# The constant products of an expert layer on Pool instead of TensorE, and a new order of DVE's steps for each expert

## What is computed

```python
xn = (x - mu) * rsqrt(var + LN_EPS) * gamma + beta
probs = softmax(xn @ Wr + br)
scores, idx = top_k(probs, 2)
full = [relu(xn @ W1_e + b1_e) @ W2_e + b2_e for each expert e]
c = einsum('ef,efh->eh', relu(b1), W2) + b2      # one row of 128 for each expert
c_total = c.sum(axis=0)
output = sum(scores * (full[idx] - c[idx] + c_total))
return residual + output
```

## Time and profile before

| | before |
|---|---|
| timed runs, median (three runs) | 3834.92 us |
| timed runs, lowest and highest | 3831.77 and 3837.63 us |
| profiled execution, its own time | 3823.62 us |
| profiled execution, span | 3821.9 us |
| mean granted clock of TensorE | 0.985 |
| PE, DVE, ACT, POOL busy | 96%, 47%, 66%, 13% |

### The profile page before, as it was taken

How to read it: one execution, slowest core, us unless ns; L and a number is a source line. 1 busy time by engine, 2 the same in 40 slices (tenths; PEclk the granted TensorE clock), 3 DMA queues, 4 the chain that set the end, 5 groups by cost and what they waited for, 6 DMA issues and landing times.

```text
span 3821.9 us, 83607 instructions
## 1 busy us (share of the span) xinstructions
PE 3665.1 (96%) x32040; PEld 1367.7 (36%) x32040; DVE 1796.6 (47%) x1809; ACT 2539.5 (66%) x2568; POOL 500.3 (13%) x1853
## 2 busy tenths in 40 slices
PE   8999999999899999999999999999999999897989
PEld 4333333334333333333333333342222223343444
DVE  3222222223377777777777777743211211443344
ACT  6999999993455555565555555479999999301321
POOL 1222222220000000000000000023322232001200
PEclk9999999999999999999999999999999999998989
DMA  6333232212111111111111110000000000000000
GB/s 194 102 83 96 79 99 81 98 72 72 58 35 38 40 38 40 38 40 38 40 38 40 39 43 1 1 23 4 4 4 4 4 30 2 17 28 0 0 13 28
DMA packets 104958, 162.88 MB, mean 43 GB/s; under 512 B 23108, under 2 KB 46048, under 8 KB 103104
## 3 DMA queue, kind: packets, MB, share of 16 engines
q1 hardware_dynamic: 104640, 158.16, 13.0%
HBM read 93.24 MB, written 64.88 MB: 41 GB/s over the span
## 4 chain that ended last, share of the span: by engine, by line
PE 76%; ACT 13%; issue 6%; DVE 4%; ACTq 1%; DMA 0%; SPq 0%; POOL 0%; DVEq 0%; POOLq 0%
PE ps L993 18%; PE ps L1018 18%; PE ps L671 10%; ACT probs L1365 7%; ACT probs L1376 5%; PE ps L603 4%; PE ps L883 3%; PE ps L493 3%; PE ps L499 3%; PE ps L1169 2%; PE ps L865 2%; PE ps L1180 2%; PE ps L1228 2%; PE ps L1242 1%; PE ps L298 1%
## 5 line engine op out<-in xcount | busy, mean ns | idle before, releaser
L1493 ACT ACTIVATE probs<-ps 128x1024 f32<-128x1024 f32 x808 | 828.3, 1025 | 586.9 <-PE ps L993 573.9
L1376 ACT ACTIVATE probs<-ps 128x1024 f32<-128x1024 f32 x1200 | 1119.4, 1032 | 50.9 <-PE ps L603 34.0
L2354 DVE TENSOR_TENSOR vbuf<-vbuf,probs 128x1024 f32<-128x1024 f32 x784 | 953.2, 1224 | 329.7 <-ACT probs L1493 329.7
L671 PE MATMUL ps<-probs,vst 128*32 128x512 f32 x6400 | 845.9, 600 | 27.1 <-ACT probs L1376 24.4
L2155 DVE COPY qs<-ps 128x512 f32<-128x512 f32 (+1 forms) x208 | 141.7, 681 | 572.4 <-PE ps L499 282.2
L1365 ACT ACTIVATE probs<-ps 128x1536 f32<-128x1536 f32 x268 | 362.0, 1624 | 9.6 <-PE ps L671 7.2
L1656 POOL CAST kst<-kb 128x128 fp32r<-128x128 f32 (+1 forms) x800 | 250.0, 313 | 746.2 <-PE ps L671 595.5
L993 PE MATMUL ps<-probs,kb 64*64 64x512 f32 x2560 | 332.2, 589 | 0.0
L1018 PE MATMUL ps<-probs,qz 64*64 64x512 f32 x2048 | 266.3, 590 | 1.8 <-DVE kb L2379 1.8
L1018 PE MATMUL ps<-probs,kb 64*64 64x512 f32 x2048 | 265.7, 589 | 0.0
L1668 POOL COPY vst<-vbuf 128x36 f32<-128x36 f32 (+1 forms) x816 | 192.4, 236 | 447.7 <-PE ps L671 441.0
(11 more groups left out here) (440 smaller groups left out, 3608.3 us busy)
## 6 DMA issues: line engine op xcount, KB each, us to landing
kv_scratch<-qs SPq DMA_DIRECT2D x192, 256.0 KB, 2.0
kb<-kv_scratch SPq DMA_DIRECT2D x72, 256.0 KB, 2.9
qz<-kv_scratch SPq DMA_DIRECT2D x56, 256.0 KB, 2.9
kb<-k_scratch SPq DMA_DIRECT2D x12, 816.0 KB, 6.9
vbuf<-in_L_ffn_W SPq DMA_DIRECT2D x32, 256.0 KB, 3.1
klo<-kv_scratch SPq DMA_DIRECT2D x32, 256.0 KB, 2.9
qs<-kv_scratch SPq DMA_DIRECT2D x32, 256.0 KB, 2.9
qz<-q_scratch SPq DMA_DIRECT2D x56, 64.0 KB, 2.1
```

Of the source, the lines that this page charges most:

```text
L671: mm = pe.matmul(ps[band, 6 + half, :], vst[:, r, band], probs[:, r, j * HT:(j + 1) * HT], start=start, stop=stop)
L1376: act.activation(probs[:, r, b * T:(b + 1) * T].rearrange("p (h n) -> p h n", h=2), ps[:, 2 * buf:2 * buf + 2, :], ACT.Exp, scale=HD8 ** - ...
L1493: act.activation(pr1[:, (u + (u == LAST1) + 2 * odd) % 4], ps[:, 2 * b:2 * b + 2, :], ACT.Exp, scale=HD64 ** -0.5)\
L2354: dve.tensor_tensor(sum1[:, odd, h], sum1[:, odd, h], e, ALU.add).then_inc(s["added"], 1)
```

## The change

Two things are changed, both in the third layer's expert part.

First, the matmuls L891 leave the experts. Pool's new function `weights8_constants` multiplies, for each expert, the second weights W2_e (128 partitions, four blocks of 128) by relu(b1_e), one value for each partition and block, and adds the product to a running sum `rbsum`; for expert 0 the product is written there directly. `rbsum` and `rbnext` lie in the free quarter of `probs`. Only then is the expert's `pick` column copied. Behind the last expert PE multiplies `rbsum` by a column of ones, four matmuls that end in column 0 of bank 7. DVE's addition of eight columns (L2547) is left out.

Second, DVE's steps are reordered. Before: weighting and sum of expert e - 1, then the four L2239 of expert e. After: weighting of e - 1, L2239 for f = 0 and 1, sum of e - 1, L2239 for f = 2 and 3. The order for m = 0 stays.

```diff
@@ PE, in expert(i, u)
-                        if h == 0 and m == 1:
-                            pe.wait_ge(s["rb_ready"], 1)
-                            for f in range(NF):
-                                pe.matmul(ps[:, 7, e:e + 1], wts[:, F + f * D:F + (f + 1) * D],
-                                          rb1[:, 0, e * NF + f:e * NF + f + 1], start=(f == 0), stop=(f == NF - 1))
@@ PE, behind the experts
             experts8(1)
+            pe.wait_ge(s["rb_ready"], 2 * E8)
+            for f in range(NF):
+                pe.matmul(ps[:, 7, 0:1], rbsum[:, f, :], ones[:, 0:1], start=(f == 0), stop=(f == NF - 1))
             pe.wait_ge(s["hid_ready"], 2 + 2 * E8 * NF)
@@ Pool, in place of weights8(1)
+            def constants8(e, u):
+
+                scales = rb1[:, 0, e * NF:(e + 1) * NF].unsqueeze(2).to_broadcast([P, NF, P])
+                kernels = vbuf[:, u * 2 * F + F:(u + 1) * 2 * F].rearrange("p (f d) -> p f d", f=NF)
+                pool.wait_ge(s[f"moe_w{u}"], e // 2 * 32 + 32 * (E8 // 2 + 1))
+                if e == 0:
+                    pool.wait_ge(s["rb_ready"], 1)
+                    pool.tensor_tensor(rbsum, kernels, scales, ALU.mult).then_inc(s["rb_ready"], 1)
+                else:
+                    pool.tensor_tensor(rbnext, kernels, scales, ALU.mult).then_inc(s["rb_ready"], 1)
+                    pool.wait_ge(s["rb_ready"], 2 * e + 1)
+                    pool.tensor_tensor(rbsum, rbsum, rbnext, ALU.add).then_inc(s["rb_ready"], 1)
+                pool.wait_ge(s["rb_ready"], 2 * e + 2)
+
+            def weights8_constants():
+
+                pool.wait_ge(s["comb_ready"], 2)
+                for e in range(E8):
+                    constants8(e, e % 2)
+                    pool.wait_ge(s["eo_ready"], e + E8 + 1)
+                    pool.tensor_copy(pick[:, e % 2:e % 2 + 1], picks[:, e:e + 1]).then_inc(s["ccol_ready"], 1)
@@ DVE, experts8(m)
+                if m == 0:
+                    for e in range(E8):
+                        weighted(e, e)
+                        accumulated(e)
+                        if e == 0:
                             context_lengths()
+                else:
+                    for e in range(E8):
+                        n = e + E8
+                        if e:
+                            weighted(n - 1, e - 1)
+                        for f in range(NF):
+                            if f == 2 and e:
+                                accumulated(n - 1)
+                            hidden8(n, e, f)
+                        if e == 0:
+                            shares8(1)
+                    weighted(2 * E8 - 1, E8 - 1)
+                    accumulated(2 * E8 - 1)
@@ DVE, behind the experts
-            then(dve.reduce_sum(stat[:, 25:26], ps[:, 7, 0:E8], AX.X))
-            then(dve.tensor_tensor(stat[:, 25:26], stat[:, 25:26], stat[:, 24:25], ALU.add))
+            then(dve.tensor_tensor(stat[:, 25:26], ps[:, 7, 0:1], stat[:, 24:25], ALU.add))
```

## The result

| | before | after |
|---|---|---|
| median of nine timed runs | 3831.66 us | 3820.20 us |
| lowest and highest | 3824.38, 3837.63 us | 3809.47, 3827.24 us |
| ratio to before, 95% interval | | 0.9969, 0.9955 to 0.9984 |
| profiled execution: time, span | 3823.62, 3821.9 us | 3827.24, 3825.5 us |
| its mean granted clock | 0.985 | 0.979 |

The change made the kernel 11.5 us faster by the medians, 0.31%. Yet its profiled execution is 3.6 us longer than the one of before: it is the slowest of the nine, while before's, at 3823.62 us, is faster than all nine timed runs of its kernel. So the two profiles must be compared stretch by stretch, and not by their ends. One timed run of the kernel before, in a later series, took 5812.54 us at a mean clock of 0.584, and is left out of the ratios.

The account below looks back on a forecast made before the run. TensorE, busy 96% of the span, was taken as the bound. Gains of 4.97 us (stalls) and 6.24 us (constants), less 0.06 us at the layer's end, made 11.15 us off 3834.92: 3823.8 us, range 3819 to 3831.

Parts of the forecast that it names:

- The hole: TensorE's stall between the two first-layer matmul halves of experts 1 to 7, waiting for DVE: 0.71 us gained each, 4.97 us together.
- f0: DVE's activation (L2239) of hidden block 0: could start 1.92 us into the expert, take 1.34 us and end at 3.26 us.
- The margin that I had put at 0.02 us: Third first-layer block's matmul ready 3.42 us into the expert, against 3.44 for the first half's end; if missed, 0.6 us gained.
- The constants: L891 leaves TensorE's queue in eight experts: 0.88 us less an uncovered 0.10 us load, so 0.78 us each, 6.24 us together.
- The end of the layer: L891's eight records run once behind the last expert, DVE's reduction L2547 falls away: 0.06 us lost, between 0 and 0.3.
- The sum: Whole-kernel total: 4.97 + 6.24 - 0.06 = 11.15 us gained, giving 3823.8 us, 0.29% less.
- Pool's operations: Fifteen new operations on 128x512 f32, eight products and seven additions, taken at 1.1 us each and off TensorE's path.
- Where Pool and DVE meet: Pool's addition and DVE's sum share a port about 5 us into an expert: 0 to 0.1 us stall in each of six experts.
- The sign of being wrong: The forecast fails if Pool's operations exceed 2 us and DVE's sum shows idle time released by Pool.
- half the gain: Rival: the stall stays (3828.7 us) or Pool holds up DVE's activations or the fourth block's input (3830.4 us); 14%.
- Pool as the bound: Rival: TensorE waits at L898 for Pool's pick column, from 15.0 us of Pool work per expert; slower, 2%.
- The clock: Rival: TensorE at 1.2 GHz for 18.8 us more matmul time turns 11.1 us gain into 7.7 us loss; 2%.

## Why the prediction was right, point by point

The mechanism was right and so was its size. In the absolute time some luck is left: 3820.2 us lies only 1.2 us inside the range, because the forecast started from a median of before that was 3.3 us too high.

**The hole.** Forecast 0.71 us for each of seven experts. With the new order alone the period fell by 0.73, from 16.49 to 15.76. The step rested on f0 starting 1.92 us into the expert, and it did, to the hundredth. The margin that I had put at 0.02 us held: the sixteen records follow one another without a gap in experts 1 to 7 of every profile with this order.

**The constants.** Forecast 0.78 us each; measured 0.79 or 0.80 for experts 1 to 7 (16.49 to 15.69). That less than the 0.88 us of L891 comes free is shown; my reason for it, that L891 had covered the weight load of L898, is not. The load's record starts together with its matmul in both kernels (the first line is of before, the second of after, timeline of PEld):

```profile
3360.41 0.18 PEld L898 LDWEIGHTS ps<-qz,pick 64*128 64x128 f32 x1
...
3358.47 0.18 PEld L894 LDWEIGHTS ps<-qz,pick 64*128 64x128 f32 x1 [0.76 <-issue]
```

For expert 0 I had charged the 0.10 us gap in front of L898 as well. There, however, L891 stood behind L898 and in front of L883, so no gap comes up: from the second half's start (3316.28 and 3322.31) to expert 1 it was 15.11 us before and is 14.22 now, 0.89 us.

**The end of the layer.** Forecast 0.06 us lost; measured 5.76 before, 5.74 after: nothing.

**The sum.** Forecast 11.15 us; in the layer it is 0.89 + 7 x 1.51 + 0.02 = 11.48, and the medians of nine runs moved by 11.46. The stretch bears the forecast out; that the medians agree to hundredths is luck, since the interval of the ratio reaches from 6 to 17 us. The forecast of 3823.8 us was 3.6 above the median of 3820.2, almost all of which is before's own median, at 3831.66 with nine runs instead of 3834.92 with three. The ratio forecast, 0.9971, stands against 0.9969.

**Pool's operations.** Forecast 1.1 us; a product takes 1.04 and an addition, whose two inputs are both full tiles, 1.27. The estimate from the Trainium skill's "GPSIMD Engine Reference", section 3.1, 1.12 us, lies between them.

**Where Pool and DVE meet.** Forecast 0 to 0.1 us in each expert; the run without products shows 0. The sum begins 4.90 us into the expert and not at 5.01, since DVE's steps overlap, so that Pool and DVE arrive within a tenth of each other and either may win. Both orders are now in the traces: Pool's addition at 2.26 us where DVE began first, DVE's sum at 2.31 us where Pool did. These two lines are of the profile of after, expert 1:

```profile
3341.38 1.26 POOL L1767 TENSOR_TENSOR probs<-probs 128x512 f32<-128x512 f32 x1
3341.42 2.31 DVE L2269 TENSOR_TENSOR work<-work 128x1024 f32<-128x1024 f32 x1
```

Whichever starts first keeps the other out until it is through: here the sum ends 1.09 us after the addition, and in expert 2 (the lines further up) the addition ends 1.11 us after the sum. The Trainium skill's "SBUF — State Buffer", section "Who interferes with whom", calls the shared port pair an exclusive lock and says that issue order decides who blocks, and here the trace agrees on both sides.

It costs no time, but the margin is small. In expert 1 the held-up sum makes the last activation end at 3346.23, 9.70 us into the expert, and the fourth matmul of the L884 block from 3343.91 (six records of 0.43 us in) reads it at about 3346.49, 0.26 us later; in expert 2, where Pool waits instead, it is about 1.3 us. I had put the activation's end at 10.0 us and the matmul at 9.9, a stall of 0.1: the end was wrong by the overlap of DVE's steps. The sign of being wrong, Pool's operations above 2 us, did come up in three of the seven additions (2.26 to 2.35 us), with three of DVE's sums at 2.28 to 2.31. It was this meeting and not slow operations, and it cost nothing.

**The rivals.** Of half the gain (14%) no part came true, and the runs exclude it: the hole closes and Pool costs nothing. Pool as the bound (2%) needs about eleven products, by the estimate above, where the change has one. The clock (2% for slower) did show in one profile, which lost 9.1 us behind the layer, but not in the median. The nine single runs lie between 10.7 us below and 7.0 us above their median; the spread of 3 us to each side that I had put down for a median fits the three medians of the changed kernel, 3819.17, 3820.20 and 3820.58 us.

## What to carry to other kernels

Where one engine is the bound and the work repeats, take one period apart into records and gaps. What leaves its queue was here worth its distance to the next record (0.88 us) less 0.09, and the edits to different parts of the period added up. Before a reordering on a second engine, write out for each step when its input is ready and when its output is wanted; the step that may wait (here the sum) goes where the next input isn't there yet, and one place too early costs 0.66 us of every period. Judge an effect of some 0.3% by the stretch that was changed and by the ratio of many runs, never by two profiles' spans.

## What the runs showed of the hardware

- TensorE's clock differs between executions of one kernel: mean 0.979 to 0.985 and 3827 to 3809 us. The same four records of L284 took 1.98 us in some executions and 3.78 in others, behind the same pause of 2.90 us.
- A pause of TensorE of 4.99 us in the middle of a busy layer was followed by a granted clock of 0.50 (3356.30 to 3361.00) and by eight records in 6.46 us instead of 3.70.
- A product of 128x512 f32 on Pool takes 1.04 us with a broadcast second operand, an addition of two full tiles 1.27 us.
- DVE with two operands in SBUF and Pool held each other up in either direction (2.31 us instead of 1.22, 2.26 instead of 1.27), but Pool, with five operations in a row and a semaphore wait between them, let DVE in behind the one that was running (2.07 us).
- Two consecutive DVE instructions overlap by 0.08 us in the profile where the second doesn't need the first's result, so a row of them is shorter than the sum of its durations. Where it does, as the sum needs the weighting, it starts 0.03 us after the other's end.
